# Second expert weights of a graph and expert kernel: scaled and split to float16 pairs during the edge stage, kept in DRAM, and multiplied in float16

## What is computed

```python
x = x + gnn(layernorm(x), src, dst, W_self, b_self, W_neigh, gamma, beta, alpha)
# experts, on t = layernorm(x):
top_vals, top_idx = top_k(t @ gate_weight.T, 2)
routing_w = softmax(top_vals)
h = silu(einsum('td,efd->tef', t, w1))              # e: 16 experts, f: 256
h_mean = masked sum of h over tokens / maximum(counts, 1)
y_mean = einsum('ef,edf->ed', h_mean, w2)           # w2: 16 x 512 x 256
x = x + routing_w times y_mean[top_idx], summed over the two picks
```

## Time and profile before

| | us |
|---|---|
| median of 3 runs (lowest, highest) | 1692.03 (1685.09, 1693.57) |
| profiled execution, own time | 1686.77 |
| its span in the profile | 1685.0 |
| PE busy | 1217.9 (72%) |
| DVE busy | 1028.5 (61%) |
| POOL busy | 992.6 (59%) |
| ACT busy | 886.9 (53%) |
| granted TensorE clock, mean of full speed | 0.887 |

### The profile page before, as it was taken

One profiled execution on the slowest core, in us unless ns is written; L12 is line 12 of the kernel. 1 busy time (PEld: TensorE's weight loads), 2 busy tenths in 40 slices (PEclk: granted clock), 3 DMA queues, 4 the chain that ended last, 5 costly groups with the idle time before them and its releaser, 6 DMA issues.

```text
span 1685.0 us, 37100 instructions
## 1 busy us (share of the span) xinstructions
PE 1217.9 (72%) x7688; PEld 644.5 (38%) x7696; DVE 1028.5 (61%) x2918; ACT 886.9 (53%) x1932; POOL 992.6 (59%) x1193
## 2 busy tenths in 40 slices
PE   4989899999665555665565546666677159999876
PEld 2545444444322222222222222234444146777612
DVE  6676235546666665657566655655658966666626
ACT  3455445555644444444444444446667838888402
POOL 2223277676777777777777777777776025555200
PEclk9999999999988888778878897799999669999885
DMA  5445277777888887888888888778877526666547
GB/s 194 141 139 166 108 219 252 243 250 225 265 265 268 264 245 237 280 260 296 261 281 279 285 279 275 240 237 249 246 233 219 216 80 201 199 200 205 192 167 275
DMA packets 141638, 384.99 MB, mean 228 GB/s; under 512 B 22911, under 2 KB 23041, under 8 KB 141509
## 3 DMA queue, kind: packets, MB, share of 16 engines
q0 software_dynamic: 75840, 248.18, 48.9%
q1 hardware_dynamic: 62392, 130.43, 21.8%
q10 hardware_dynamic: 3276, 4.97, 0.9%
HBM read 323.78 MB, written 59.72 MB: 228 GB/s over the span
## 4 chain that ended last, share of the span: by engine, by line
PE 39%; POOL 24%; issue 16%; DVE 9%; DMA 7%; POOLq 2%; SPq 2%; ACT 1%; DVEq 0%; ACTq 0%
POOL work L617 24%; PE ps L861 13%; PE ps L960 10%; PE ps L1053 6%; DMA work<-table,work 4%; PE ps L1064 3%; PE ps L1055 3%; POOLq L612 2%; PE ps L1113 1%; SPq L525 1%; DMA work<-in_w_t 1%; DMA work<-in_x 1%; PE ps L907 1%; DVE slots L1515 1%; PE ps L934 1%
## 5 line engine op out<-in xcount | busy, mean ns | idle before, releaser
L617 POOL DMA_INDIRECT work<-table,work x832 | 828.4, 996 | 295.6 <-issue 239.8
L960 PE MATMUL ps<-work 128*128 x2056 | 574.6, 431 | 345.0 <-DMA work<-table,work 329.5
L960 PEld LDWEIGHTS ps<-work 128*128 128x128 f16 x2056 | 216.4, 106 | 589.9 <-issue 445.3
L715 ACT ACTIVATE work<-work,ones 128x512 f16<-128x512 f16 x259 | 185.3, 715 | 325.7 <-PE ps L963 325.2
L709 ACT ACTIVATE work<-iota_row,work 128x128 f16<-128x128 f32 x1040 | 331.3, 390 | 31.6 <-ACT work L715 23.9
L861 PE MATMUL ps<-wparts,slots 128*128 128x512 f16 x1176 | 274.1, 383 | 12.2 <-DVE slots L1251 12.2
L1339 DVE TENSOR_SCALAR inv<-ps 128x1 f32 (+2 forms) x49 | 7.7, 158 | 336.6 <-PE ps L963 331.9
L633 POOL DMA_INDIRECT slots<-x_d,betab x114 | 107.8, 946 | 161.8 <-PE ps L1064 83.9
L861 PEld LDWEIGHTS ps<-wparts,slots 128*128 128x128 f16 x1176 | 115.8, 99 | 139.8 <-DVE slots L1251 14.7
L1053 PE MATMUL ps<-work,wparts 128*128 x456 | 156.1, 382 | 2.2 <-ACT wparts L801 2.0
L801 ACT COPY wparts<-ps 128x1024 f16<-128x1024 f16 x114 | 115.3, 1012 | 59.8 <-PE ps L1064 59.1
(11 more groups left out here) (283 smaller groups left out, 1577.5 us busy)
## 6 DMA issues: line engine op xcount, KB each, us to landing
work<-in_x SPq DMA_DIRECT2D x96, 256.0 KB, 2.8
work<-in_w_t SPq DMA_DIRECT2D x48, 512.0 KB, 7.6
work<-table,work POOLq DMA_INDIRECT x832
table<-work SPq DMA_DIRECT2D x48, 256.0 KB, 2.0
x_d<-work SPq DMA_DIRECT2D x48, 256.0 KB
x_d<-slots SPq DMA_DIRECT2D x48, 256.0 KB
out_x<-slots SPq DMA_DIRECT2D x48, 256.0 KB
slots<-x_d SPq DMA_DIRECT2D x41, 256.0 KB
```

Source lines behind the costliest of these rows:

```text
L617: pool.indirect_dma_start(out=gath[:, g % GRING, w, :], out_offset=None, in_=table[:, :], in_offset=bass.IndirectOffsetOnAxis(ap=idx_all[: ...
L715: act.activation(hot[:, slot, :, :], away[:, slot % 2, :, :], ACT.Relu, bias=ones[:, 0:1], scale=-1.0).then_inc(c_hot, 1)
L960: pe.matmul(ps[:, ds(bank, 1), :], hot[:, s, w, :], gath_row[:, ds(at + (2 * w + half) * D, D)].unsqueeze(1), start=False, stop=True, skip ...
```

## The change

The second expert weights w2 get what the first ones have. In tiles 0 to 15 SP also loads one expert's w2 (512 KB) into `raw2`, a part of the weight buffer that is free by then, and DVE takes its maximum. After that both maxima go through DRAM and both scales are made. In tiles 20 to 35 w2 is loaded again, DVE scales it to a high and a low float16 half, and SP stores the pair to the new DRAM tensor `w2s_d`. The pair of w2 is written over `stage`, the place of the raw w1 of the same tile; so the load of the next w1 now waits until the store of the w2 pair has landed (`u_st`), where it waited for the split of w1 before.

At the end the loads of w2 take rows of 4 KB from `w2s_d` instead of 2 KB rows from the input; their number and bytes are the same. `diag` becomes a float16 pair, and PE makes two float16 products where it made one float32 product. The factor 1/count moves from after the product into the means; for that, two small DVE operations move ahead of the wait for the map, and one small product on PE, one small DVE operation to make its operand and one to take its result are added in the routing.

```diff
             def load_split(it, b):
                 j = HALF * it + b
-                sp.wait_ge(v_split, j - SPLIT_AT + 1)
+                sp.wait_ge(u_st, 16 * (j - SPLIT_AT + 1))
...
+            def load_split2(it, b):
+                j = HALF * it + b
+                sp.wait_ge(u_split, j - SPLIT_AT + 1)
+                sp.nop(nofuse=True)
+                sp.dma_start(raw2[:, :, :].rearrange("p c n -> p (c n)"), w2_t[ds((j - SPLIT_AT) * P, P), :]).then_inc(u_ld, 16)
...
+            def store_split2(it, b):
+                j = HALF * it + b
+                sp.wait_ge(u_split, j - SPLIT_AT + 2)
+                sp.nop(nofuse=True)
+                sp.dma_start(w2s_d[ds((j - SPLIT_AT) * P, P), :], stage_halved[:, :, :, :].rearrange("p c a n -> p (c a n)")).then_inc(u_st, 16)
...
                     if split:
                         load_split(it, b)
+                        load_split2(it, b)
                     store_x1(it, b)
                     store_x2(it, b)
                     if split:
                         store_split(it, b)
+                        store_split2(it, b)
...
             for e in range(EXPERTS):
-                sp.dma_start(w2[:, e, :, :], w2_t[e, :, :].rearrange("(c p) n -> p c n", p=P)).then_inc(g_w2[e // 4], 16)
+                sp.dma_start(w2[:, e, :, :, :].rearrange("p c a n -> p (c a n)"), w2s_d[e * P:(e + 1) * P, :]).then_inc(g_w2[e // 4], 16)
...
                 for c in range(FF // P):
-                    last = pe.matmul(ps[0:EXPERTS, 0, :], diag[:, c, e, :], w2[:, e, c, :],
-                                     start=e == 0 and c == 0, stop=e == EXPERTS - 1 and c == FF // P - 1)
+                    pe.matmul(ps[0:2 * EXPERTS, 0, :], diag[:, c, e, :, :].rearrange("p a f -> p (a f)"), w2[:, e, c, 0, :],
+                              start=e == 0 and c == 0, stop=False, skip_group_check=True)
+                    last = pe.matmul(ps[0:EXPERTS, 0, :], diag[:, c, e, 0, :], w2[:, e, c, 1, :], start=False,
+                                     stop=e == EXPERTS - 1 and c == FF // P - 1, skip_group_check=True)
...
                     dve.tensor_reduce(wmax[:, ds(j + 3, 1)], flat(stage[:, :, :]), X, ALU.max,
                                       apply_absolute_value=True).then_inc(v_max, 1)
+                    dve.wait_ge(u_ld, 16 * (j + 1))
+                    dve.tensor_reduce(wmax[:, ds(j + 3 + EXPERTS, 1)], flat(raw2[:, :, :]), X, ALU.max,
+                                      apply_absolute_value=True).then_inc(u_max, 1)
...
                     dve.scalar_tensor_tensor(halved[:, :, 1, :], stage[:, :, :], wscale[:, 3:4], halved[:, :, 0, :],
                                              ALU.mult, ALU.subtract).then_inc(v_split, 1)
+                    dve.wait_ge(u_ld, 16 * (j - SPLIT_AT + EXPERTS + 1))
+                    dve.nop(nofuse=True)
+                    dve.wait_ge(v_split, j - SPLIT_AT + 2)
+                    dve.nop(nofuse=True)
+                    dve.tensor_scalar(stage_halved[:, :, 0, :], raw2[:, :, :], wscale[:, 9:10], None, ALU.mult).then_inc(u_hi, 1)
+                    dve.wait_ge(u_hi, j - SPLIT_AT + 1)
+                    dve.nop(nofuse=True)
+                    dve.scalar_tensor_tensor(stage_halved[:, :, 1, :], raw2[:, :, :], wscale[:, 9:10], stage_halved[:, :, 0, :],
+                                             ALU.mult, ALU.subtract).then_inc(u_split, 1)
...
+            ln.link(dve.tensor_scalar(es[0:EXPERTS, 4:5], es[0:EXPERTS, 0:1], 1.0, None, ALU.max))
+            ln.link(dve.reciprocal(es[0:EXPERTS, 5:6], es[0:EXPERTS, 4:5]))
+            dve.wait_ge(e_base, 1)
+            dve.tensor_scalar(kbase[:, :], ident[0:EXPERTS, 0:EXPERTS], es[0:EXPERTS, 5:6], None, ALU.mult).then_inc(e_inv, 1)
             dve.wait_ge(i_map, 1)
...
             dve.wait_ge(g_sum, 1)
+            ln.link(dve.tensor_tensor(means, ps[:, 7, 0:2 * EXPERTS].rearrange("p (c e) -> p c e", c=2),
+                                      share_of.unsqueeze(1).to_broadcast([P, 2, EXPERTS]), ALU.mult))
+            ln.link(dve.tensor_copy(mean16[:, 0, :, :], means))
+            ln.link(dve.tensor_tensor(mean16[:, 1, :, :], means, mean16[:, 0, :, :], ALU.subtract))
             for c in range(FF // P):
-                last = dve.tensor_tensor(diag[:, c, :, :], same,
-                                         ps[:, 7, c * EXPERTS:(c + 1) * EXPERTS].unsqueeze(2).to_broadcast([P, EXPERTS, EXPERTS]),
-                                         ALU.mult)
+                for a in range(2):
+                    last = dve.tensor_tensor(diag[:, c, :, a, :], same,
+                                             mean16[:, a, c, :].unsqueeze(2).to_broadcast([P, EXPERTS, EXPERTS]), ALU.mult)
```

## The result

The changed kernel takes 1697.49 us (median of 9 runs, 1695.38 to 1701.45), the kernel before 1689.28 us (9 runs, 1685.09 to 1693.57): ratio 1.0056, 95% interval 1.0041 to 1.0071. The forecast was 1702, with "slower" the likeliest. The medians differ by 8.2 us; the profiled executions have spans of 1693.6 and 1685.0 us and differ by 8.6 us.

What follows compares the result with a forecast made beforehand. It took POOL's gathers to bound the edge stage. +14 us there and -4 us at the end, added to the three-run median of 1692.0, gave 1702 us; range 1688 to 1712.

Steps and rivals of the forecast that it cites:

- The second hold: Tiles 20 to 35: new two-input DVE operation holds a next gather 1.98 us, not 0.95; +14 us, ends 0 and 16.5.
- 12 tiles at 1.03 and 4 at 0.4: Edge stage, 16 split tiles: added gather time in us per tile, the 4 being tiles with late second loads; +14 us.
- The one-input scaling: Edge stage, DVE's scaling in the split: claimed not to hold a gather, as read from L1379 in the earlier trace.
- scaling too: Rival, edge stage: the held gather stays held through new scaling and new two-input operation, 36.5 us more; 1725; chance 0.05.
- second hold missed: Rival, edge stage: next gather starts under 0.10 us into the new operation and runs through; 1690, not slower; chance 0.20.
- SP, transfers, DVE's tile: Edge stage, split tiles: more transfers and DVE's 2.3 us of added work per tile cost nothing.
- Maxima: Edge stage, early tiles: w2's reduction of 1.21 us holds no gather; 0 us, upper end 2 us.
- Routing: Routing: added small DVE operations and PE product are covered by waits; 0 us, without that cover 0.5 to 1 us.
- The end: Last product: load 1.4 us earlier, last quarter 5 us instead of 7.05; -4 us, ends 0 and -9.
- no gain at the end: Rival, last product: load ends as late as before, PE's clock fallen, 6.9 us replace 7.05; 1707; chance 0.08.

Runs made afterwards that it cites:

- the one-input run: Changed kernel with w2's low half written by a one-input DVE operation instead of a two-input one (values wrong); ratio 1.0010 to the kernel before.
- 0.49 us of delay on DVE: Changed kernel with an unused reduction of 256 columns put on DVE ahead of the second scaling; ratio 0.9977 to the kernel before.
- the product alone: Kernel before with only the float16 product at the end, loading stored w1 pairs, no w2 work in the edge stage; ratio 0.9939 to the kernel before.
- the kernel with four pieces: Changed kernel with both two-input operations of a split cut into four pieces of 256 columns; 1669.61 us, ratio 0.9877 to the kernel before.
- the one with one-input operations cut too: Changed kernel with all two-input operations of the edge stage cut, and its larger one-input ones in two pieces each; ratio 0.9825 to the kernel before.

## Why the prediction came out as it did

The sign was right, and the time 4.5 us too high against 1697.49. Of these, 2.7 us are the base: I added to a median of three runs, 1692.03, and nine runs give 1689.28. The sum itself, +10, stands against 8.2 us between the medians and 8.6 between the profiles. Both of its terms were too small, with opposite signs: stage 18.7 where I had 14, end -8.2 where I had -4. Their errors of 4 to 5 us each nearly cancelled, so it is partly luck that the sum came so close; the mechanism of the hold, and not its count, is what was right.

*The second hold.* Its mechanism was right. In a tile I had 1.76 + 1.98 = 3.74 us for the two gathers and the trace has 1.93 + 1.80 = 3.73. The 16 tiles' long gathers lie 29.0 us over 0.947 each in the changed kernel and 12.9 before: 16.1 us, practically the upper end of 16.5. The mis-sized step was "12 tiles at 1.03 and 4 at 0.4": there were no tiles with late weights. Some 2.5 us more came from other gathers, and it looks like scatter: all other gathers of over 1.0 us add up to 30.8 us over 0.947 against 27.7 before, and the kernel that only had its rows widened at the end shows 31.5.

*The one-input scaling.* The reading of the earlier trace rows was wrong, as the one-input run showed, and with it the statement that the fast one-input form doesn't take the lock. It did no harm to the sum, since in the changed kernel no gather begins in L1430: the first, held by L1424, ends behind it. The rival "scaling too" failed on that: a held gather isn't passed on whole to the next operation, it ended only 0.16 us later. But the rival "second hold missed" was right about its point of decision (it lies at 0.07 us, inside my 0.04 to 0.10). Its 0.03 to 0.09 us of margin were 0.21 to 0.27 us, as the first gather's 0.16 us moved the second further in; 0.49 us of delay on DVE (750.66 less 749.20, against 750.81 less 749.84) made it true, at 0.9977.

*SP, transfers, DVE's tile.* Nothing, as predicted. The DMA share rose to 0.92 over 800 to 1000 us with 311 to 314 GB/s, POOL's gaps stayed at 0.30 us, and DVE still waited 279.5 us in all for PE ahead of L1378. *Maxima:* nothing; 16 gathers of the changed kernel began in the new L1414, and each took 0.94 to 0.95 us. *Routing:* 0.8 us where I had 0, within its bound without cover.

*The end.* Two sizes were off. The last landing came 5.6 us earlier, not 1.4. I had scaled all bytes by the rates of the earlier trace rows; but the 30 us from the first issue moved 369 GB/s before and 378 after (0.3 MB), while another 0.44 MB before trickled in over the next 6 us at 74 GB/s. Here are these windows, of before and of after, columns as above:

```profile
1585.44:1615.44 30.00, 29.08 (x100) 14.59 (x100) 6.95 (x14) 0.00 (x0) 0.00 (x0) 0.77 1.04 369
1615.44:1621.44 6.00, 4.67 (x11) 0.87 (x9) 0.00 (x0) 0.00 (x0) 0.00 (x0) 1.00 0.21 74
```
```profile
1603.15:1633.15 30.00, 25.95 (x111) 18.19 (x111) 8.26 (x19) 0.00 (x0) 0.00 (x0) 0.67 0.99 378
1633.15:1639.15 6.00, 4.74 (x18) 1.71 (x18) 0.74 (x1) 0.00 (x0) 0.00 (x0) 1.00 0.07 26
```

The width of the rows is what did it: the kernel before with that edit alone had its last landing after 31.0 us, and over all traces it came after 30.4 to 31.7 us in the nine kernels with rows of 4 KB and after 35.6 to 36.0 us in the three with rows of 2 KB. And the last quarter took 3.67 us at 1.00 instead of the 5 that I took between 3.5 and 6.9. That was this execution's luck, since other traces with the same product took up to 6.5 us, so 5 was no bad guess; -8.2 stands for this one profile. With 5.6 + 3.4 = 9.0 the gain stood at the bound of -9. The rival "no gain at the end" was wrong.

What stays open: what sets the clock of the last quarter; why the product alone gained more in the medians (9.2 us) than in its profile (3.6 us of span), beyond the profiled execution's being one of its longer ones; and why 17 gathers of the changed kernel that began 0.05 to 0.07 us into L1406 took 1.06 us, neither free nor held to its end.

## What to carry to other kernels

Where GpSimd's gathers set the time, read VectorE's operations above each long one and note where in them it began: one that starts from about 0.1 us into a long SBUF operation on, and at least 0.13 us before its end, is held to that end; one that starts earlier mostly runs through. Such operations are here those with two inputs in SBUF and the one-input scalings and shifts; the reductions of 1.21 us held none. Cut such operations into short pieces before moving work under them; here pieces of 256 columns cost VectorE 0.4 us each time and took 28 us off the stage (1113.8 to 1085.9). A change can be worth doing and still measure slower: cost its two halves apart, and time each alone.

## What was not expected of the hardware

- A held gather ended 0.82 us behind the end of the operation in which it began, for two-input operations of 0.75 and 1.29 us and for the one-input operation of 0.75 us alike. An undisturbed one takes 0.95 us, so a gather that began in an operation's last 0.13 us was not delayed. The Trainium skill (SBUF — State Buffer, on the two separate sides) gives about 115 ns from the operation's end to the release; no run here shows it or excludes it, since a held step that comes later in the gather would fit the same rows with it.
- Operations that follow each other don't hold as one: behind a split in four pieces no gather took over 1.05 us, behind the whole operations 1.93 and 1.80 us, and an operation 0.10 us behind the first added only 0.16 us.
- 16 loads of 512 KB took SP 20.8 to 21.8 us to issue with rows of 2 KB (three kernels) and 11.4 to 12.6 us with rows of 4 KB (nine kernels).
- PE's clock was at 2.4 GHz for the last products after an idle time of 2.21 us and at 1.2 GHz after 3.71 us, in two kernels with the same loads; the idle time alone doesn't decide it, for after 3.52 us it stood at 1.2 GHz in the kernel with four pieces and at 2.4 GHz in the one with one-input operations cut too.
